# A gate worked in chunks of seven tiles, with expert token lists from one-hot matmuls and rows gathered by the experts stage

## What is computed

```python
xn = layernorm(x)
gate_logits = xn @ gate_w + gate_b                  # 16 experts
topk_vals, topk_idx = jax.lax.top_k(gate_logits, 2)
topk_w = jax.nn.softmax(topk_vals, axis=-1)
h = relu(einsum('bsh,ehf->bsef', xn, w1) + b1)      # F = 512
expert_out = einsum('bsef,efh->bseh', h, w2) + b2   # only the two chosen are needed
y = xn + sum(topk_w * chosen expert_out)
x = x + layernorm(y) * gamma + beta
```

## Time and profile before

| what | us |
|---|---|
| three runs: median (lowest to highest) | 2828.68 (2823.84 to 2830.24) |
| the profiled execution | 2825.55 |
| its span in the profile | 2823.5 |
| PE, PEld busy | 2306.0, 1929.9 |
| DVE, ACT, POOL busy | 1478.0, 896.3, 1620.7 |
| indirect gathers of the edge aggregation (L868), POOL | 775.4 |
| PE hidden layer and output of the experts (L1635, L1642) | 207.8 and 199.7 |

### The profile page before, as it was taken

One profiled execution on the slowest core, in us unless ns is written; L12 is line 12 of the kernel. 1 busy time (PEld: TensorE's weight loads), 2 busy tenths in 40 slices (PEclk: granted clock), 3 DMA queues, 4 the chain that ended last, 5 costly groups with the idle time before them and its releaser, 6 DMA issues. The chain is left out here.

```text
span 2823.5 us, 50917 instructions
## 1 busy us (share of the span) xinstructions
PE 2306.0 (82%) x12841; PEld 1929.9 (68%) x12842; DVE 1478.0 (52%) x4377; ACT 896.3 (32%) x2710; POOL 1620.7 (57%) x2170
## 2 busy tenths in 40 slices
PE   7877777788888666555499999799979999994798
PEld 7655665566666554455488888677758999993798
DVE  8645544445455544478422222277757777776311
ACT  2431222222222111134233333266653433341233
POOL 4837777777777777757564000187856555550233
PEclk9989889888888766855699999899999999996899
DMA  4043333333333333312333333222231111111122
GB/s 153 15 123 103 101 101 102 100 101 101 103 102 102 102 101 103 100 53 87 126 101 115 108 124 114 86 72 73 74 93 37 44 42 45 43 45 52 27 36 31
DMA packets 149395, 235.70 MB, mean 83 GB/s; under 512 B 28475, under 2 KB 110096, under 8 KB 149330
## 3 DMA queue, kind: packets, MB, share of 16 engines
q0 software_dynamic: 55856, 141.65, 17.9%
q1 hardware_dynamic: 77218, 73.40, 8.1%
q10 hardware_dynamic: 16256, 19.93, 2.1%
HBM read 175.04 MB, written 59.82 MB: 83 GB/s over the span
## 5 line engine op out<-in xcount | busy, mean ns | idle before, releaser
L868 POOL DMA_INDIRECT all_XN<-h_table,l_srcI x784 | 775.4, 989 | 244.2 <-issue 237.5
L1068 PE MATMUL gcn_acc<-all_XN,gcn_hot 128*128 128x256 f32 x800 | 264.1, 487 | 130.5 <-DMA all_XN<-h_table,l_srcI 113.7
L1068 PE MATMUL gcn_acc<-all_XN 128*128 128x256 f32 x768 | 250.4, 483 | 117.0 <-DMA all_XN<-h_table,l_srcI 101.3
L1068 PEld LDWEIGHTS gcn_acc<-all_XN,gcn_hot 128*128 128x128 f32 x800 | 182.5, 239 | 192.7 <-issue 100.6
L1068 PEld LDWEIGHTS gcn_acc<-all_XN 128*128 128x128 f32 x768 | 173.1, 236 | 174.3 <-issue 91.2
L1741 POOL DMA_INDIRECT comb_ys<-slots_out,all_slot x98 | 100.2, 1022 | 311.2 <-POOLq L1488 287.9
L1560 ACT ACTIVATE moe_hidden<-moe_hid_ps,moe_b 128x128 f32<-128x128 f32 x420 | 130.7, 364 | 301.2 <-PE moe_hid_ps L1635 301.2
L1635 PEld LDWEIGHTS moe_hid_ps<-moe_xst,moe_w 128*128 128x128 f32 x1680 | 204.4, 193 | 28.2 <-issue 22.1
L1635 PE MATMUL moe_hid_ps<-moe_xst,moe_w 128*128 128x128 f32 x1680 | 207.8, 277 | 17.2 <-issue 16.1
L969 DVE COPY_PREDICATED gcn_last_seen<-gcn_seen_sb,gcn_seen 128x392 f32<-128x392 int32 x98 | 57.6, 587 | 288.2 <-ACT gcn_seen_sb L802 288.2
L802 ACT COPY gcn_seen_sb<-gcn_seen 128x392 f32<-128x392 f32 x98 | 47.6, 486 | 505.4 <-PE gcn_seen L1075 505.4
(11 more groups left out here) (386 smaller groups left out, 4916.3 us busy)
## 6 DMA issues: line engine op xcount, KB each, us to landing
moe_w<-in_e_w ACTq DMA_DIRECT2D x32, 512.0 KB, 4.4
moe_xs<-slots_in SPq DMA_DIRECT2D x106, 128.0 KB
slots_out<-moe_y SPq DMA_DIRECT2D x105, 128.0 KB
all_XN<-h_table,l_srcI POOLq DMA_INDIRECT x784, 2.7
all_X<-in_x SPq DMA_DIRECT2D x7, 896.0 KB, 11.2
z_table<-comb_zb SPq DMA_DIRECT2D x49, 128.0 KB
x_table<-all_XN SPq DMA_DIRECT2D x49, 128.0 KB, 1.7
out<-all_X SPq DMA_DIRECT2D x49, 128.0 KB, 1.7
```

Of the source, the lines that this page charges most:

```text
L868: nc.gpsimd.indirect_dma_start(msg[b][:, c, :], None, self.h_table, bass.IndirectOffsetOnAxis(self.srcI[:, GE * g + c:GE * g + c + 1], 0)) ...
L1068: last = nc.tensor.matmul(acc[b % NA][:, :], hot[b % NH][:, c, :], msg[b][:, c, :], start=(c == 0), stop=(c == GE - 1))
```

## The change

The gate stage and the experts stage become one scope, `moe_stage`, with a clear of the semaphores and a barrier between the two parts as before. The gate works on chunks of seven tiles: statistics, root, inverse, top-2 selection and ranks are taken for seven tiles at once, all without hardware loops. ACT applies the layernorm straight into XN. Nothing is scattered and nothing filled: SP stores XN, chunk by chunk, in a plain table `rows_table`. From rank and first tile each node's slot is split into tile (of 115) and lane (of 128); one-hot matrices of both, in bfloat16, are multiplied on PE, so that each slot receives the number of its node, in two parts, as 98 matmuls of 256 columns that add up in one PSUM bank. The transposed result, `listed`, holds a column of row numbers per tile. The first two experts' weights are loaded by SP during the gate.

In the experts stage POOL gathers 128 rows of `rows_table` by a column of `listed` into a half of `ring`, and DVE copies that half into xs. POOL's loop goes over pairs of tiles and holds the look-up and keep of one node tile per pair. A gather waits for the landing of the gather before it. SP only stores.

```diff
@@ gate: SP, POOL, ACT @@
+                    self.weights(sp, 0, 0)
+                    self.weights(sp, 1, 1)
+                    for c in range(C):
+                        sp.wait_ge(xn_ready, CT * c + CT)
+                        sp.dma_start(self.rows_table[CT * P * c:CT * P * (c + 1), :].rearrange("(c p) d -> p c d", p=P),
+                                     XN[:, CT * D * c:CT * D * (c + 1)].rearrange("p (c d) -> p c d", d=D)).then_inc(rows_out, 16)
...
+                    for c in range(C - 1):
+                        pool.wait_ge(placed, PL * c + PL)
+                        nc.gpsimd.tensor_tensor(tables[:, c, 1, :, :], low[c % 2][:, :, :], tile_no[:, c, :].unsqueeze(1).broadcast_to([P, P, PC]), ALU.mult).then_inc(low_t, 1)
...
+                    def by_lane(c):
+                        act.wait_ge(placed, PL * c + PL)
+                        nc.scalar.activation(tables[:, c, 0, :, :], low[c % 2][:, :, :], ACT.Copy, scale=self.place_no).then_inc(low_p, 1)
+
+                    for c in range(C):
+                        root(c)
+                        if c >= 3:
+                            by_lane(c - 3)
+                        apply(CT * c)
+                        for t in range(CT * c + 1, CT * c + CT):
+                            apply(t)
+                            copy_xxt(t - 1)
+                        copy_xxt(CT * c + CT - 1)
@@ gate: DVE, some of the 14 top-2 and 8 placing instructions @@
+                            nc.vector.tensor_reduce(top_v[:, k, tiles_in(c)], (less if k else logits)[:, :, :], AX_X, ALU.max).then_inc(chosen, 1)
+                            nc.vector.tensor_tensor(marked[:, :, :], (less if k else logits)[:, :, :], of_tile(top_v[:, k, tiles_in(c)]), ALU.is_equal).then_inc(chosen, 1)
...
+                            nc.vector.tensor_tensor(own_rank[:, :, :, :], pick[:, c, :, :, :], rank_ps[c % 2][:, :, :].unsqueeze(1).broadcast_to([P, 2, CT, E]), ALU.mult).then_inc(placed, 1)
...
+                            nc.vector.tensor_tensor(low[c % 2][:, :, :], lane[:, :].unsqueeze(1).broadcast_to([P, P, PC]), iota_pc[:, :, :], ALU.is_equal).then_inc(placed, 1)
...
+                    for c in range(1, C + 2):
+                        f, g = c - 2, c - 3
...
+                        take(f)
+                        scales(c)
+                        carry(f)
...
+                    link(nc.vector.tensor_tensor(start_each[:, :, :], pick[:, :, :, :, :].rearrange("p c k t e -> p (c k t) e"),
+                                                 start_b[:, :].unsqueeze(1).broadcast_to([P, 2 * T, E]), ALU.mult))
+                    link(nc.vector.tensor_reduce(self.start_of[:, :], start_each[:, :, :], AX_X, ALU.add))
...
+                    for c in range(C):
+                        after(dve, high_used, c - 1)
+                        nc.vector.tensor_tensor(high[c % 2][:, :, :], tile_of[:, c, :].unsqueeze(1).broadcast_to([P, MAX_TILES, PC]), iota_pc[:, 0:MAX_TILES, :],
+                                                ALU.is_equal).then_inc(high_ready, 1)
@@ gate: PE @@
+                        nc.tensor.matmul(ranks[:, :, :], before[:, :], taken[:, c, 0:CT, :], start=True, stop=False)
+                        for later in range(1, CT):
+                            nc.tensor.matmul(ranks[:, later:CT, :], ones[:, :], taken[:, c, 0:CT - later, :], start=False, stop=False)
...
+                        for i in range(PC):
+                            last = nc.tensor.matmul(list_ps[0:MAX_TILES, :, :], high[c % 2][:, :, i], tables[:, c, :, :, i],
+                                                    start=(c == 0 and i == 0), stop=(c == C - 1 and i == PC - 1))
@@ experts: SP @@
-                    def load(i):
-                        after(sp, turned_ready, i)
-                        row = sp.value_load(self.tile_row[0:1, ds(i, 1)], min_val=0, max_val=E * (ROWS + P) - P)
-                        sp.dma_start(xs[:, :], self.slots_in[ds(row, P), :]).then_inc(xs_in, 16)
@@ experts: POOL @@
+                    def gather(i, p):
+                        after_alone(pool, self.passed, ring_in, 16 * i)
+                        after_alone(pool, self.passed, xs_ready, i - 1)
+                        nc.gpsimd.tensor_copy(row_1[p][:, :], self.listed[:, ds(i, 1)]).then_inc(row_1_ready, 1)
+                        after_alone(pool, self.passed, row_1_ready, i + 1)
+                        nc.gpsimd.indirect_dma_start(ring[:, p * D:p * D + D], None, self.rows_table,
+                                                     bass.IndirectOffsetOnAxis(row_1[p][:, :], 0)).then_inc(ring_in, 16)
...
+                    gather(0, 0)
+                    gather(1, 1)
+                    pool.wait_ge(key_chain, 7)
+                    look_up(0)
+                    with pool.Fori(1, T) as h:
+                        gather(2 * h, 0)
+                        keep(h - 1)
+                        look_up(h)
+                        gather(2 * h + 1, 1)
+                    keep(T - 1)
+                    with pool.Fori(T, npairs) as h:
+                        gather(2 * h, 0)
+                        gather(2 * h + 1, 1)
@@ experts: DVE @@
+                    def take(i):
+                        after(dve, ring_in, 16 * i + 16)
+                        after(dve, turned_ready, i)
+                        nc.vector.tensor_copy(xs[:, :], ring[:, ds((i % 2) * D, D)]).then_inc(xs_ready, 1)
...
                             turn(i + 1)
+                            take(i + 2)
                             after(dve, y_done, i + 2)
                             after(dve, y_out, 16 * i + 16)
                             nc.vector.tensor_tensor(y[:, :], y_ps[:, :], b2[p][:, :], ALU.add).then_inc(y_ready, 1)
```

More of the change, by code:

```diff
@@ L1225, in gate_stage @@
[L1225 to L1234 removed]
+            pairs = s.sb("pairs", [1, 1])
@@ L1286, in _, with root, apply @@
-                    staggered(act, [(2, half(root)), (3, half(copies)), (8, copy_rows)], T, NB)
-                    fill(act, E // 2, E)
+                    def root(c):
+                        act.wait_ge(var_ready, CT * c + CT)
+                        nc.scalar.activation(sd[:, tiles_in(c)], mv[:, tiles_in(c), 1], ACT.Sqrt, bias=self.eps).then_inc(sd_ready, 1)
+                    def apply(t):
+                        act.wait_ge(shift_ready, t // CT + 1)
+                        nc.scalar.activation(XN[:, D * t:D * t + D], X[:, D * t:D * t + D], ACT.Identity, bias=shift[:, t:t + 1], scale=rs[:, t:t + 1]).then_inc(xn_ready, 1)
@@ L1288, in _ @@
+                    for c in range(C - 3, C - 1):
+                        by_lane(c)
                     act.wait_ge(gap_ready, 1)
-                    nc.scalar.activation(gap_e[:, :], gap[:, :], ACT.Exp).then_inc(gap_exp, 1)
+                    nc.scalar.activation(self.gap_e[:, :], gap[:, :], ACT.Exp).then_inc(gap_exp, 1)
+                    by_lane(C - 1)
                 @block.vector
@@ new lines, in _, with bias @@
+                    each = [P, CT, E]
+                    of_all = lambda v: v.unsqueeze(1).broadcast_to(each)
+                    of_tile = lambda v: v.unsqueeze(2).broadcast_to(each)
+                    def bias(c):
+                        if 0 <= c < C:
+                            dve.wait_ge(logit_done, CT * c + CT)
+                            after(dve, chosen, CH * c)
+                            nc.vector.tensor_tensor(logits[:, :, :], logit_ps[c % 2][:, :, :], of_all(gate_b[:, :]), ALU.add).then_inc(chosen, 1)
@@ L1390, in _ @@
[L1390 to L1397 removed]
+                    lane_number(c)
@@ new lines, in _ @@
+                    pe.wait_ge(consts_in, 48)
+                    pe.wait_ge(ready, 5)
+                    for c in range(C):
+                        if c >= 2:
+                            rank(c - 2)
+                        turn(CT * c)
+                        for t in range(CT * c + 1, CT * c + CT):
+                            turn(t)
+                            gate(t - 1)
+                        gate(CT * c + CT - 1)
+                    rank(C - 2)
+                    rank(C - 1)
```

554 lines of the change are left out of this document (307 added, 247 removed).

## The result

The changed kernel takes 2884.93 us (median of 4 runs, 2881.29 to 2886.35) against 2829.46 for the kernel before, measured beside it: a ratio of 1.0198, 95% interval 1.018 to 1.0216. It is **2% slower**, 55 us, where 2818 was forecast, and it lies above the range, which ended at 2858. The profiled execution has a span of 2883.0 against 2823.5.

The account below looks back on a forecast made before the run. DVE was taken to bound the gate and PE the experts. From 2825.55 us, 61 came off for the gate and 51 were added for the experts, giving 2815.5; with 3.1 added 2818.6, so 2818, range 2765 to 2858.

Parts of the forecast that it names:

- what bounds each stage: Before: DVE bounds the gate, PE the experts; after: POOL bounds the experts, 8.9 us a pair against PE's 7.46.
- The start up to gather 2: Experts stage: gather 2 is issued 8.8 us after the stage begins.
- The last ones: End of the experts stage: the last eight gathers come 4.15 us apart, 33 us.
- signs of being wrong: Wrong if POOL idles before copies waiting for take, gathers land later than 2.8, or gate chunks exceed 11.2 us.
- Step 1: Experts stage: weight loads collide with gathers at 14 experts, 0.5 us each, 7 us.
- Rival D: Experts stage: gathers land behind weights, about 5 in place of 2.75, 28 times, 63 us; total 2874; chance 0.12.
- Step 2: End of the experts stage: POOL's last gather ends the block 1.3 us later than the store did.
- Step 3: Gate's list: 98 matmuls of 256 bf16 columns at 0.17 us each, 17 us, range 11 to 28.
- Step 4: Gate chunk: POOL's product over 1792 numbers, at most 5.0 us, is hidden by the chunk.
- rival E: Experts stage: DVE's take copy, 0.29 us, holds up POOL's issue of 106 gathers, 31 us; total 2849; chance 0.06.
- Rival C: Gate: clock stays at 0.50 since transposes don't count for it; stage takes 118 us, total 2829; chance 0.20.
- my mean of 84 and 99: Gate before the list: 84 us at full clock, 99 at the lower, two thirds of the time at full clock.

Follow-up runs that it names:

- experiments 2: Changed kernel with one-hots and tables of the list stage laid out so list matmuls read and load neighbouring columns: 2857.11 us, ratio 1.0111.
- experiment 10: Changed kernel with neighbouring columns only on the moving side of the list matmuls, loaded one-hots still stepped by 28 bytes: 2895.95 us, one execution.
- experiment 1: Changed kernel with a semaphore per ring half, POOL passing a landing on after issuing the next gather: 2796.14 us, ratio 0.9894.
- experiment 8: Changed kernel with POOL's loop of 48 pairs written out, so its waits are on constants; wait for each landing kept: 2800.47 us, ratio 0.9921.
- experiment 4: Changed kernel without the weight loads of 14 experts, which run with the weights of the first two: 2855.18 us, one execution.
- the best: Changed kernel with landings passed on later, neighbouring list columns on both sides, and DVE's statistics beside POOL's product: 2762.95 us, ratio 0.9773.

## Why the prediction was wrong

**What held.** The list of what bounds each stage was right: POOL took over from PE in the experts, by the landing, the look-up and the register waits in a cycle of 8.9 us (measured 8.9 to 9.0 in most pairs), with the 4.75 and 4.15 in it. The start up to gather 2 was 8.7 us (8.8 worked out). The last ones came 4.0 to 5.0 apart (4.15). The removal of 98 scatters and the per-tile chain did shorten the gate. And all that was forecast as untouched is unchanged within 1.3 us. One of the signs of being wrong that I had named came true: gathers that land later than 2.8.

**Step 1 that failed: the weights that collide with gathers, "an estimate of 0.5 each, 7 us".** It was 2.6 for each of 14, and the stage without the loads is 32.3 us shorter. The estimate came from the median of the earlier trace rows, 2.8, which leaves out exactly the gathers that matter; its maximum of 7.0 stood in the same row. Rival D had the mechanism with 63 us and a chance of 0.12: it took two gathers per load where it is one, at a landing nearly as I had priced it. A median is the wrong number for a term that occurs once per expert.

**Step 2: the end of the stage.** I closed the block 1.3 us after the old store would have. It is about 5 more (8.6 us from the start of the last y to the combine, against 2.6 before): the last gather is taken into no tile, yet the block waits for it and for POOL's drain of 3.74. A drain of 4.98 had been there before, at 1527, under 288 us of cover, and I put it at nothing without saying what would cover it now.

**Step 3: the list, "I take 0.17, 17 us", bounds 0.11 and 0.29.** Measured 0.47, outside the bounds, 46 us in place of 17: the largest miss of all, 29 us. The lower bound came from 49 stepped columns and the upper from 256 columns at the slower clock, which assumes one column a cycle; nothing in the trace of before showed a wide matmul with a stepped moving operand, and I treated the step as free. With neighbouring columns it is 0.21 at the lower clock, at what the upper bound says without a load. Only experiments 2 and 10 show that the step is the cause. The 0.08 for a load in the upper bound stands in no row; a stepped load took 0.28 to 0.30 here. And the nearest row was stepped too, by 32 bytes and not by 28: its matmuls start 0.11 apart at clock 1.00, and its loads of 128 columns take 149 ns in the mean, where the stepped loads of 114 columns in experiment 10 take 0.30. Whether the length of the step, not only its presence, makes this difference was not tried.

**Step 4: "POOL's product over 1792 numbers ... hidden by the chunk".** Its 3.35 us were under the 5.0 of the bound, but it isn't beside DVE's work, it stops it: the engine's time was counted, and not what two engines share. 6.5 us. I had looked at this very interference (rival E) for the wrong pair of instructions. The take's copy and POOL's issue do overlap, in 41 cases in the changed kernel: the take stays at 0.29 to 0.30 and the issue at 0.98. In other kernels it is the take that suffers: beside an issue it takes up to 0.53 in experiment 1 (9 of 20 overlaps are longer than 0.31) and up to 0.51 in experiment 8, and beside POOL's addition of beta up to 0.84, while the issue there stays at 0.97 to 1.00. Rival E had it the other way round, POOL held up by the take's 0.29. The Trainium skill, SBUF — State Buffer, Who interferes with whom, has both rules, that of a copy, which I cited, and that of a DVE instruction with two SBUF inputs, which bites here.

**Rival C's condition came true, its price did not.** The clock stayed at 0.50 throughout, and with the stall out of the way the list begins at 88.5 us, where my mean of 84 and 99, with two thirds of the time at the full clock, had 89. That hit is luck: the clock was wrong, and for the clock that was granted the sum said 99, a figure whose steps I hadn't written down. It was too long by about as much as the wrong clock took off; part of that is the chunk, 10.2 and not 11.2. The rival's reason falls: the clock didn't rise when the transposes were replaced by matmuls.

Summed: list +29, stall +6.5, weights +25 (the 32 of experiment 4 for 7), end of the stage +5, is 66 of the 67 between 2818 and 2885. That it comes out so closely is in part chance, since the 89 above is. All four have one sign. My range treated the unknown costs as if they could cancel, and let none of them leave its bounds; yet three of the four were added work of a kind that the trace of before did not show beside other work.

## What to carry to other kernels

Added work is priced from its nearest row in shape, and the access pattern is a part of the shape: a step in a matmul's moving operand, a repeated innermost operand on DVE and a stepped write each cost a factor here, from 1.9 to over 7, and no instruction count shows it. For an engine that issues gathers, add up what stands between two issues, landing and waits included, and hold it against the period of the engine that it feeds. Telling it of a landing after it has issued the next gather was worth 89 us of the 122 between the changed kernel and the best; cheaper waits in the old order were worth 84. Before work is moved to an idle engine, ask what that engine shares with the busy one, and at the end of a block ask which engine drains last.

## What the runs showed of the hardware

- A list matmul of 256 bf16 columns, 28 bytes apart, starts every 0.47 us at clock 0.50; with neighbouring columns every 0.21 at 0.50 and 0.11 at 1.00. With neighbouring moving columns and a load of 114 columns 28 bytes apart (0.30 us) it is 0.21 at either clock.
- The granted clock stayed at 0.50 for 46 us in which PE was 99% busy with stepped matmuls, and for 40 us in which it was 94% busy with plain matmuls, 84 of 193 of them of 16 columns. It rose to 1.00 in the course of the list when the moving columns were neighbours, with stepped loads or not. How the clock is decided was not tried further and stays open.
- A wait on a register's value ahead of an indirect DMA, with the increment that the helper puts behind it, costs about 0.5 us more than one on a constant: 0.79 to 0.81 against 0.27 to 0.31.
- A gather issued 0.3 to 1.1 us behind a weight load of 1.1 MB was taken 2.6 us later than the others; the next gather was late by 0.6 us once and else on time.
- A DVE product of two SBUF tensors begun beside POOL's product ends 0.12 to 0.13 us after POOL's (3.15 us for 0.26), while statistics, aggregates and maxima beside it keep their time. DVE's f32 copy of 256 numbers was held in some overlaps with POOL's DMA issue (up to 0.53 for 0.29, experiments 1 and 8) and not in others.
- Writing 1792 bf16 numbers 512 bytes apart takes 8.1 to 8.3 us on ACT, POOL and DVE alike, where they take 1.1 to 3.4 in the other two layouts.
